# Perceiver block, flash attention over 25088 keys: the probabilities' transposes moved from TensorE to DMA and VectorE

## The chip, the core and the metric

The kernel runs on one core of a Trainium2 chip. The metric is the time of one execution on the device in microseconds; three executions of the kernel before took 2474.32, 2474.45 and 2477.35 us (median 2474.45).

## The reference

Inputs in float32: x [1, 256, 2048] and a context [1, 25088, 2048]. Three residual layers follow each other:

```python
x = x + xattn(layernorm(x), ctx)      # softmax(q @ ctx.T) @ ctx: the context is keys and values at once
x = x + attn(layernorm(x), Wq, bq, Wk, bk, Wv, bv)   # small attention inside each token, 32 heads, 8 kv heads
x = x + ffn(layernorm(x), W_base, b_base, W_gate, A, B)  # base matmul and 2 of 8 low-rank experts
```

The first layer has 256 queries against 25088 keys with 2048 dimensions and takes most of the time; only its loop is changed.

## The kernel before, in words

**Number format.** Every float32 operand is split into a rounded part ("hi", cast by ScalarE) and the difference ("lo", by VectorE or GpSimd). `product` (L1488 ff.) then takes three matmuls, hi x hi, hi x lo and lo x hi, of 128 x 128 by 512 columns (L1491 to L1493).

**Blocks and turns.** The keys are read in 49 blocks of 512. A *turn* is the work of one block, and each engine has its own program of turns, tied by semaphores. The block comes from memory twice: as `quart` (32 x 32 blocks are turned by VectorE, L1081, into the `tr` chunks: 16 chunks of 128 dimensions, the scores' operand) and as `raw` (natural rows, the values' operand, in four pieces of 512 columns).

**TensorE** in one turn: `chunk_scores` for 16 chunks (six matmuls each: two query tiles by three), and between them the weighted sums of the block *before*: eight pieces (two query tiles by four column pieces) of 12 matmuls. PIECE_AFTER (L414) says after which chunk a piece comes; pieces 6 and 7 are late and come after chunks 0 and 1 of the next turn (LATE_AFTER, L415). After chunk 1 and the late pieces stand the eight transposes of the probabilities of the block before (`probs_group`, L1543, four of 128 x 128 for each query tile, into PSUM).

**ScalarE**: the hi cast of each chunk (L770, may be three chunks ahead; a chunk's cast needs the chunk four before to be used up), after that of chunk 3 the exponentials of both query tiles (`softmax`, L783), after that of chunk 5 the hi part of the turned probabilities (L754), and the hi parts of the value pieces (L781): pieces 2 and 3 of the block before after chunks 3 and 7, pieces 0 and 1 of this block after chunks 11 and 15 (ROWS, L804).

**VectorE** in `iteration` (L1159): the row maxima, then for chunks 3 to 18 (16 to 18 are 0 to 2 of the next turn) the difference `lo_chunk` (L1085) and the block transpose of the chunk three ahead (L1081); after chunk 5 the differences of the probabilities (`pt_lo`, L1026), after chunk 7 `rescale` (two operations on 128 x 2 numbers, L1114 and L1116), and after the chunks in ADD_AFTER and ADD_LATE_AFTER (L1141) the additions of finished pieces to `acc` (L1124, L1133). An addition frees the PSUM bank that the piece after next writes.

**GpSimd**: the differences of the value pieces (`lo_piece`, L617, four operations of 128 x 512 each, L621), always in the order 0, 1, 2, 3 of a block. In the first 16 turns after the first it also loads and sums a piece of Wq and stores it (L634 to L643), in the others it sums a window of W_base in every second turn (L649).

**SyncE** issues nearly all loads and stores in order, each with its wait in front (`next_block`, L488). In the last turns it also issues the eight loads of the experts' matrix B (`load_expert`, L521): four after the next-to-last block's loads, four after the load of x for the second layer (`x_nat`), ahead of the last block's pieces 2 and 3.

## Time and profile before

| | |
|---|---|
| median of three executions | 2474.45 us |
| profiled execution, its own time | 2480.7 us |
| its span, first to last instruction | 2478.9 us |
| TensorE (PE) busy | 2444.7 us, 99% |
| VectorE (DVE) busy | 1966.2 us, 79% |
| GpSimd (POOL) busy | 1412.2 us, 57% |
| ScalarE (ACT) busy | 1098.5 us, 44% |
| mean granted TensorE clock | 0.996 |
| mean DMA rate | 210 GB/s |

How to read it: PE is the matmuls, PEld the weight loads that lie beside them, DVE VectorE, ACT ScalarE, POOL GpSimd, SP SyncE; a name with q, as SPq, is an engine's queue, which issues DMAs. Matmuls are pipelined, so the distance between two starts, not the duration of one, is what a matmul costs. L621 is line 621 of the kernel before. Idle time of an engine that is not the bound costs nothing.

### The profile page before, as it was taken

The numbers are of one execution on the slowest core, as the hardware profiler recorded it, in microseconds if no ns is written. First come the engines' busy times: TensorE is split into PE (matmuls) and PEld (weight loads), VectorE is DVE, ScalarE is ACT, GpSimd is POOL, SyncE is SP. The second block draws the span as 40 slices with busy tenths as digits, with TensorE's granted clock in tenths as the row PEclk, the third lists the DMA queues.
The fourth block names the chain that finished last, engine by engine and source line by source line (L and its number), as shares of the span: only waits on it lengthen the run. The fifth ranks groups of instructions, "written<-read, shape, count | busy, mean of one in ns | idle before, by whom it ended". The sixth has DMA issues, their size and how long they took to land. (4 is left out here: it accounts for less than half of the span.)

```text
span 2478.9 us, 36112 instructions
## 1 busy us (share of the span) xinstructions
PE 2444.7 (99%) x11446; PEld 2013.8 (81%) x11446; DVE 1966.2 (79%) x2706; ACT 1098.5 (44%) x1577; POOL 1412.2 (57%) x1052
## 2 busy tenths in 40 slices
PE   6999999999999999999999999999999999999999
PEld 5888888888888888888888888888888888877777
DVE  8888788787888888888888888888888888874456
ACT  4444444444444444444444444444444444433543
POOL 2766666666665655655566565556556555651541
PEclk9999999999999999999999999999999999999999
DMA  9988878888789888889888988888888898789642
GB/s 231 257 221 213 233 203 230 218 208 230 205 231 230 213 204 219 217 220 217 209 220 206 226 217 203 219 223 210 215 217 220 214 216 215 201 187 189 173 119 90
DMA packets 434167, 519.80 MB, mean 210 GB/s; under 512 B 66886, under 2 KB 308550, under 8 KB 431688
## 3 DMA queue, kind: packets, MB, share of 16 engines
q1 hardware_dynamic: 424136, 477.23, 79.0%
q0 software_dynamic: 9984, 41.95, 5.2%
q8 instruction: 28, 0.46, 0.1%
q14 instruction: 19, 0.16, 0.0%
HBM read 488.71 MB, written 30.41 MB: 209 GB/s over the span
## 5 line engine op out<-in xcount | busy, mean ns | idle before, releaser
L621 POOL TENSOR_TENSOR nat_lo<-raw,nat_hi 128x512 fp32r<-128x512 f32 x784 | 1171.0, 1524 | 862.7 <-ACT nat_hi L781 829.7
L1085 DVE TENSOR_TENSOR ch_lo<-tr,ch_hi 128x512 fp32r<-128x512 f32 x784 | 762.6, 973 | 295.5 <-ACT ch_hi L770 291.7
L770 ACT CAST ch_hi<-tr 128x512 fp32r<-128x512 f32 x784 | 481.3, 621 | 797.7 <-PE ps L1493 777.3
L1491 PE MATMUL ps<-ch_hi,xt_hi 128*128 128x512 f32 x1696 | 671.7, 396 | 9.3 <-DVE ch_lo L1085 5.1
L1493 PE MATMUL ps<-ch_hi,xt_lo 128*128 128x512 f32 x1696 | 662.1, 390 | 0.0
L1492 PE MATMUL ps<-ch_lo,xt_hi 128*128 128x512 f32 x1696 | 661.5, 390 | 0.0
L1491 PE MATMUL ps<-nat_hi,pt_hi 128*128 128x512 f32 x1568 | 610.4, 389 | 0.0
L1493 PE MATMUL ps<-nat_hi,pt_lo 128*128 128x512 f32 x1568 | 610.3, 389 | 0.0
L1492 PE MATMUL ps<-nat_lo,pt_hi 128*128 128x512 f32 x1568 | 610.0, 389 | 0.0
L1081 DVE STREAM_TRANSPOSE tr<-quart 128x512 f32<-128x512 f32 x784 | 547.5, 699 | 2.4 <-DMA quart<-in_ctx_dram 2.2
L781 ACT CAST nat_hi<-raw 128x2048 fp32r<-128x2048 f32 x196 | 374.4, 1910 | 207.5 <-PE ps L1493 186.2
L1491 PEld LDWEIGHTS ps<-ch_hi,xt_hi 128*128 128x128 f32 x1696 | 319.1, 188 | 76.5 <-issue 6.5
L1493 PEld LDWEIGHTS ps<-ch_hi,xt_lo 128*128 128x128 f32 x1696 | 319.0, 188 | 67.5
L1492 PEld LDWEIGHTS ps<-ch_lo,xt_hi 128*128 128x128 f32 x1696 | 319.3, 188 | 63.0
L1491 PEld LDWEIGHTS ps<-nat_hi,pt_hi 128*128 128x128 f32 x1568 | 294.4, 188 | 61.4 <-DVE pt_lo L1026 0.4
L1493 PEld LDWEIGHTS ps<-nat_hi,pt_lo 128*128 128x128 f32 x1568 | 294.3, 188 | 61.1
L1492 PEld LDWEIGHTS ps<-nat_lo,pt_hi 128*128 128x128 f32 x1568 | 294.4, 188 | 60.9
L1124 DVE SCALAR_TENSOR_TENSOR acc<-acc,alpha,ps 128x512 f32<-128x512 f32 x240 | 170.0, 708 | 16.2 <-PE ps L1493 16.1
L1133 DVE SCALAR_TENSOR_TENSOR acc<-acc,alpha,ps 128x512 f32<-128x512 f32 x144 | 103.2, 717 | 4.4 <-PE ps L1493 4.4
L754 ACT CAST pt_hi<-ps 128x512 fp32r<-128x512 f32 x98 | 52.8, 589 | 116.3 <-PE ps L1500 116.3
L1026 DVE TENSOR_TENSOR pt_lo<-ps,pt_hi 128x512 fp32r<-128x512 f32 x98 | 63.1, 685 | 49.0 <-ACT pt_hi L754 49.0
L787 ACT ACTIVATE probs<-ps,neg_max 128x512 f32<-128x512 f32 x98 | 67.2, 686 | 73.8 <-DVE neg_max L1106 73.8
(202 smaller groups left out, 1387.0 us busy)
## 6 DMA issues: line engine op xcount, KB each, us to landing
quart<-in_ctx_dram SPq DMA_DIRECT2D x392, 512.0 KB, 8.4
raw<-in_ctx_dram SPq DMA_DIRECT2D x196, 1024.0 KB, 8.2
wq_in<-in_L_attn_Wq_dram POOLq DMA_DIRECT2D x16, 1024.0 KB, 6.3
win<-in_L_ffn_W_base_dram SPq DMA_DIRECT2D x64, 256.0 KB, 6.8
tr<-wt_dram POOLq DMA_DIRECT2D x64, 256.0 KB, 3.6
wt_dram<-stage SPq DMA_DIRECT2D x32, 256.0 KB, 5.6
wt_dram<-stage_b SPq DMA_DIRECT2D x32, 256.0 KB, 10.3
wq_dram<-wq_out POOLq DMA_DIRECT2D x16, 256.0 KB, 2.3
```

Of the source, the lines that this page charges most:

```text
L621: last = pool.tensor_tensor(nat_lo[:, j, t], raw[:, j % 2, t], nat_hi[:, j, t].bitcast(F32), ALU.subtract)
L770: act.copy(ch_hi[:, c % RING_CH, :], tr[:, c % RING_TR, :]).then_inc(chunk_hi, 1)
L781: act.copy(nat_hi[:, j], raw[:, j % 2]).then_inc(nat_hi_ready, 1)
L787: act.activation(probs[:, q, :], ps[:, SCORE_BANK + TT * new + q, :], ACT.Exp, bias=neg_max[:, new, q:q + 1], accum_out=row_sum[:, q:q + 1 ...
L1026: dve.tensor_tensor(dst, src, hi.bitcast(F32), ALU.subtract).then_inc(lo_drained, 1)
L1081: dve.transpose(tr[:, c % RING_TR, :].rearrange("p (r i) -> p r i", i=SQ), src).then_inc(chunk_transposed, 1)
L1085: dve.tensor_tensor(ch_lo[:, c % RING_CH, :], tr[:, c % RING_TR, :], ch_hi[:, c % RING_CH, :].bitcast(F32), ALU.subtract).then_inc(chunk_s ...
L1124: dve.scalar_tensor_tensor(piece, piece, alpha[:, 1 - turn.parity, q:q + 1], ps[:, out_bank(v, turn.over), :], ALU.mult, ALU.add).then_inc ...
L1133: dve.scalar_tensor_tensor(piece, piece, alpha[:, turn.parity, q:q + 1], ps[:, out_bank(v, False), :], ALU.mult, ALU.add).then_inc(acc_upd ...
L1491: pe.matmul(out_, a_hi, b_hi, start=start, stop=False)
L1492: pe.matmul(out_, a_hi, b_lo, start=False, stop=False)
L1493: return pe.matmul(out_, a_lo, b_hi, start=False, stop=stop)
```

## The change

In turns 2 to 48 of the loop (`by_dma`: neither first, second nor the closing one) the probabilities are no longer turned by TensorE. ScalarE writes them with their columns permuted in groups of 32. GpSimd, on its own DMA queue, issues eight DMAs from `probs` to a new buffer `quads`, each of 128 rows of 128 numbers, that deal the 128 partitions out to groups of 32 partitions (`move_next_probs`). VectorE then does two 32 x 32 block transposes of 128 x 512 back into `probs` (`turn_probs`); their output goes to every fourth word. The hi and lo parts are taken from `probs` in SBUF and no longer from PSUM. GpSimd's order becomes pieces 0 and 1, the moves for the next turn, pieces 2 and 3. In front of the moves of each tile stands a one-column multiply (`beat`) that waits for the exponential.

With it change: the places of TensorE's pieces 0 and 1 (after chunks 6 and 8, before 5 and 7), of two casts and two additions, the order of addition, turned probabilities and chunk transpose in VectorE's loop; piece 0 waits for the first tile's probabilities only, and piece 1 for the second's. As `quads` takes the room of the experts' B matrix, all eight of its loads now come after `x_nat` and wait for the last probabilities.

```diff
...
         b_nat = put(at_b, "b_nat", [P, DC, ER])
+        quads = put(at_b, "quads", [P, TT, QR, P])
         x1_sum = put(at_b, "x1_sum", [P, TT, QKC])
...
         ones = sb("ones", [P, P])
+        beat = sb("beat", [P, 1])
         early_exp = sb("early_exp", [P, 1])
...
         probs_ready = sem("probs_ready")
+        beat_done = sem("beat_done")
+        probs_moved = [sem(f"probs_moved{q}") for q in range(TT)]
         alpha_ready = sem("alpha_ready")
...
                 self.second = isinstance(i, int) and 2 * i + 1 + step == 1
+                self.by_dma = not (self.first or self.second or self.over)
...
-        PIECE_AFTER = {5: 0, 7: 1, 9: 2, 11: 3, 13: 4, 15: 5}
+        PIECE_AFTER = {6: 0, 8: 1, 9: 2, 11: 3, 13: 4, 15: 5}
         LATE_AFTER = {0: 6, 1: 7}
...
             next_block(REST[0], LAST_M)
-            for e in range(EXPERTS // 2):
-                load_expert(e)
...
             sp.dma_start(x_nat[:], x_dram).then_inc(x_again, 16)
-            for e in range(EXPERTS // 2, EXPERTS):
+            sp.wait_ge(lo_drained, G_PT + TT * (NB - 1))
+            for e in range(EXPERTS):
                 load_expert(e)
...
                 pool.memset(neg_max[:, parity, :], -LOWEST).then_inc(max_ready, 1)
+            pool.memset(beat[:, :], 1.0).then_inc(beat_done, 1)
             pool.memset(denom[:, :], 0.0).then_inc(denom_ready, 1)
...
                     lo_piece(j, turn.times(PIECES, j + 1))
+
+            def move_next_probs(turn, q):
+
+                pool.wait_ge(beat_done, turn.times(TT, q - 1))
+                pool.wait_ge(probs_ready, turn.times(TT, q + 1))
+                pool.tensor_tensor(beat[:, :], ones[:, 0:1], ones[:, 0:1], ALU.mult).then_inc(beat_done, 1)
+                for b in range(QR):
+                    pool.dma_start(quads[b * SQ:(b + 1) * SQ, q], probs[:, q, b * P:(b + 1) * P]).then_inc(probs_moved[q], 16)
...
                     split_block(Turn(i, step), range(2))
+                    for q in range(TT):
+                        move_next_probs(Turn(i, step), q)
                     pool.wait_ge(wq_loaded, i * 32 + 16 * step + 16)
...
                     sum_win(m)
-                split_block(turn)
+                split_block(turn, range(2))
+                if not turn.last:
+                    for q in range(TT):
+                        move_next_probs(turn, q)
+                split_block(turn, range(2, PIECES))
...
                 act.wait_ge(max_ready, turn.times(TT, q + 1))
-                act.activation(probs[:, q, :], ps[:, SCORE_BANK + TT * new + q, :], ACT.Exp,
+                to, of = probs[:, q, :], ps[:, SCORE_BANK + TT * new + q, :]
+                if turn.by_dma:
+                    to = to.rearrange("p (b t j) -> p t b j", b=QR, t=KT)
+                    of = of.rearrange("p (t b j) -> p t b j", b=QR, t=KT)
+                act.activation(to, of, ACT.Exp,
                                bias=neg_max[:, new, q:q + 1],
...
             def probs_group(turn, q):
-                hi_group(turn.times(TT, G_PT + q - TT), q, pt_hi[:, q], bank4(q))
+                if turn.by_dma:
+                    act.wait_ge(out_ready, turn.times(8, 6 + q + 1 - 16))
+                    hi_group(turn.times(TT, G_PT + q - TT), q, pt_hi[:, q], probs[:, q].rearrange("p (t m) -> p t m", t=KT))
+                else:
+                    hi_group(turn.times(TT, G_PT + q - TT), q, pt_hi[:, q], bank4(q))
...
             SECOND_ROWS = {15: 0, 18: 1}
-            ROWS = {11: 0, 15: 1}
+            ROWS = {12: 0, 15: 1}
...
+            def turn_probs(turn, q):
+
+                dve.wait_ge(probs_moved[q], turn.times(16 * QR, -16 * QR))
+                dve.transpose(probs[:, q].rearrange("p (t i a) -> p t a i", t=KT, a=QR),
+                              quads[:, q].rearrange("p a (t j) -> p t a j", t=KT)).then_inc(group_done, 1)
+
             def probs_group(turn, q):
-                lo_group(turn.times(TT, G_PT + q - TT), pt_lo[:, q], bank4(q), pt_hi[:, q])
-
-
-
-            ADD_AFTER = {9: 0, 11: 1, 13: 2, 15: 3, 17: 4}
+                src = probs[:, q].rearrange("p (t m) -> p t m", t=KT) if turn.by_dma else bank4(q)
+                lo_group(turn.times(TT, G_PT + q - TT), pt_lo[:, q], src, pt_hi[:, q])
+
+
+
+            ADD_AFTER = {10: 0, 12: 1, 13: 2, 15: 3, 17: 4}
             ADD_LATE_AFTER = {3: 5, 5: 6, 7: 7}
...
                     lo_chunk(turn.times(DC, c), c)
+                    if c in ADD_LATE_AFTER and lagging:
+                        add_late_piece(turn, ADD_LATE_AFTER[c])
+                    if c == (7 if turn.second else 5) and not turn.first:
+                        if turn.by_dma:
+                            for q in range(TT):
+                                turn_probs(turn, q)
+                        for q in range(TT):
+                            probs_group(turn, q)
                     n = c + AHEAD
...
                         transpose_chunk(turn.times(DC, n), n, turn.times(16 * QR, 16 * QR * (n // DC)))
-                    if c == (7 if turn.second else 5) and not turn.first:
-                        for q in range(TT):
-                            probs_group(turn, q)
-                    if c in ADD_LATE_AFTER and lagging:
-                        add_late_piece(turn, ADD_LATE_AFTER[c])
                     if c == 7 and not turn.first:
...
                     pe.wait_ge(lo_drained, turn.times(TT, G_PT - 1 + (v > 0)))
+                elif turn.by_dma and v < TT:
+                    pe.wait_ge(lo_drained, turn.times(TT, G_PT - 1 + v))
                 elif v == 0:
...
                         late_piece(turn, LATE_AFTER[c])
-                    if c == (3 if turn.second else 1) and not turn.first:
+                    if c == 3 and turn.second:
                         for q in range(TT):
```

## Rows read from the trace of the kernel before

**Rows 1.** The page: engines' busy time with instructions, and the SyncE DMA queue.
```profile
PE 2444.7 (99%) x11446; PEld 2013.8 (81%) x11446; DVE 1966.2 (79%) x2706; ACT 1098.5 (44%) x1577; POOL 1412.2 (57%) x1052
...
q1 hardware_dynamic: 424136, 477.23, 79.0%
```

**Rows 2.** Time line of TensorE: start, duration in us, line, operation, count.
```profile
1521.12 1.03 PE L1500 MATMUL ps<-ident,probs 128*128 128x128 f32 x8
...
1523.37 0.39 PE L1491 MATMUL ps<-ch_hi,xt_hi 128*128 128x512 f32 x1
...
1544.90 0.39 PE L1493 MATMUL ps<-nat_hi,pt_lo 128*128 128x512 f32 x1
...
2010.63 0.47 PE L1491 MATMUL ps<-ch_hi,xt_hi 128*128 128x512 f32 x1
...
2055.07 0.48 PE L1491 MATMUL ps<-ch_hi,xt_hi 128*128 128x512 f32 x1
```

**Rows 3.** Waits, 100 to 2150 us: total, times, longest.
```profile
DVE ch_lo L1085 <- ACT ch_hi L770: 281.5, 257, 4.1
```

**Rows 4.** Time line of VectorE in the same turn, idle time before in brackets.
```profile
1519.30 1.47 DVE L1085 TENSOR_TENSOR ch_lo<-tr,ch_hi 128x512 fp32r<-128x512 f32 x1 [0.27 <-ACT ch_hi L770]
1520.70 0.70 DVE L1081 STREAM_TRANSPOSE tr<-quart 128x512 f32<-128x512 f32 x1
...
1527.62 1.19 DVE L1114 TENSOR_TENSOR denom_s<-denom,alpha 128x2 f32<-128x2 f32 x1
1528.85 1.21 DVE L1116 TENSOR_TENSOR denom<-denom_s,row_sum 128x2 f32<-128x2 f32 x1
```

**Rows 5.** Groups by form: busy us, mean ns of one, idle time before.
```profile
L1085 DVE TENSOR_TENSOR ch_lo<-tr,ch_hi 128x512 fp32r<-128x512 f32 x784 | 762.6, 973 | 295.5 <-ACT ch_hi L770 291.7
...
L1026 DVE TENSOR_TENSOR pt_lo<-ps,pt_hi 128x512 fp32r<-128x512 f32 x98 | 63.1, 685 | 49.0 <-ACT pt_hi L754 49.0
```

**Rows 6.** Time line of ScalarE in the same turn.
```profile
1513.72 0.19 ACT L787 ACTIVATION_READ_ACCUMULATOR probs<-ps,neg_max 128x1 f32 x1
...
1518.65 0.62 ACT L770 CAST ch_hi<-tr 128x512 fp32r<-128x512 f32 x1 [2.23 <-PE ps L1493]
...
1525.51 1.91 ACT L781 CAST nat_hi<-raw 128x2048 fp32r<-128x2048 f32 x1
```

**Rows 7.** Time line of GpSimd: same turn, and four DMA issues after the loop.
```profile
1515.98 5.94 POOL L621 TENSOR_TENSOR nat_lo<-raw,nat_hi 128x512 fp32r<-128x512 f32 x4 [5.67 <-ACT nat_hi L781]
...
2218.22 2.14 POOL L685 DMA_DIRECT2D tr<-wt_dram  x4
```

**Rows 8.** The page's DMA issues: count, KB each, median us to landing.
```profile
tr<-wt_dram POOLq DMA_DIRECT2D x64, 256.0 KB, 3.6
wt_dram<-stage SPq DMA_DIRECT2D x32, 256.0 KB, 5.6
...
wq_dram<-wq_out POOLq DMA_DIRECT2D x16, 256.0 KB, 2.3
```

**Rows 9.** Groups by form: strided outputs (L639, L923) and a plain one (L758).
```profile
L639 POOL TENSOR_TENSOR wq_in<-wq_in 128x512 f32<-128x512 f32 x16 | 17.7, 1104 | 0.0
...
L758 ACT COPY att_t<-ps 128x512 f32<-128x512 f32 x16 | 9.3, 580 | 0.0
...
L923 ACT COPY v_t<-ps 64x256 f32<-64x256 f32 x8 | 5.0, 630 | 0.1
```

**Rows 10.** Time lines of SyncE's queue, GpSimd and TensorE around the last block.
```profile
2133.36 7.83 SPq L522 DMA_DIRECT2D b_nat<-in_L_ffn_B_dram  x4
...
2156.55 12.10 SPq L522 DMA_DIRECT2D b_nat<-in_L_ffn_B_dram  x4
...
2172.95 0.43 SPq L436 DMA_DIRECT2D raw<-in_ctx_dram  x1
...
2182.90 10.51 POOL L621 TENSOR_TENSOR nat_lo<-raw,nat_hi 128x512 fp32r<-128x512 f32 x8 [7.12 <-ACT nat_hi L781]
...
2193.96 0.39 PE L1491 MATMUL ps<-nat_hi,pt_hi 128*128 128x512 f32 x1
```

## The prediction

> **What bounds the kernel now.** I read the page first: engines' busy time, the DMA queues, the granted clock. TensorE is busy 99% of the span and the queue of SyncE alone takes 79% of the 16 DMA engines [rows 1]. Then TensorE's time line over one turn, because a busy share does not say whether the matmuls follow each other without a gap. They do: from the matmul at 1523.37 to the one at 1544.90 there are 95 starts, 0.2266 us each [rows 2], at a granted clock near 1. A turn (one block of 512 keys) has 16 chunks x 6 and 8 pieces x 12 = 192 matmuls, 192 x 0.2266 = 43.51 us. The turn itself, from the chunk 2 matmul at 2010.63 to the same one at 2055.07, is 44.44 us [rows 2]. The 0.93 us between are the eight transposes and the slower restart behind them. So in the loop TensorE is the only bound; the other engines wait for it (VectorE for ScalarE's casts 281.5 us, and these for TensorE's freed chunks) [rows 3].
>
> I count times from S, the first matmul of chunk 0 of a turn. The transposes start 36 matmuls later, S + 8.16, and do so at 1521.12 [rows 2], so in the traced turn S = 1512.96.
>
> **Part 1: the eight transposes go.** Turns 2 to 48 are changed, 47 of them: 47 x 0.93 = 43.7 us less on TensorE, if nothing makes it wait. The first two and the closing turn keep them.
>
> **Part 2: the new way of the probabilities.** ScalarE's second exponential is through at 1513.91, S + 0.95 [rows 6], the first 0.86 earlier, S + 0.1. The permuted views cost ScalarE nothing that I count: runs of 32 words, same number of elements. GpSimd, whose piece 1 is done before S, now issues two small multiplies and eight DMAs. Four back to back took 2.14 us [rows 7]; with about 0.1 for each multiply (my guess, no row shows it) the last issue starts at S + 4.1 and ends at S + 4.7. The landing: 2.3 us for the SBUF store on this queue, 3.6 for a load on it [rows 8]. So the last block lands at S + 6.4 to 7.7. Behind these issues wait, on GpSimd, the differences of piece 2, before at 1515.98 = S + 3.0 [rows 7], now at about S + 5, until S + 11. TensorE needs piece 2 only after chunk 13, and the reload of the raw buffer behind it has over 10 us of cover, so the 2 us are hidden. In the 16 turns with the Wq sums, these come behind the moves too and push piece 2 to S + 12; the raw reload then comes about 3 us late for its cast, and the idle time of GpSimd before piece 1 takes that up.
>
> **Part 3: VectorE.** This is where the gain can be lost. TensorE without transposes reaches chunk 8 after 84 matmuls, S + 19.03 (before: after chunk 7, piece 1 and piece 0, far later), because pieces 0 and 1 now stand behind chunks 6 and 8. VectorE's chain to the difference of chunk 8 begins with that of chunk 5, which can't start before chunk 1 is used: 1519.30 = S + 6.34 [rows 4]. Then, by start-to-start times (an instruction's duration less 0.07 that the next one overlaps):
> - the chunk 5 difference 1.40 [rows 4]
> - two late additions, the transposes of chunks 8, 9, 10 and the two new ones, seven at 0.70 less 0.07: 7 x 0.63 = 4.41 (the chunk transpose's 0.70 stands for the new ones) [rows 4]
> - the two denominator steps 1.19 and 1.21, to the next start 2.36 [rows 4]
> - five differences: probabilities 0 and 1, chunks 6, 7 and 8. A difference of two SBUF tiles takes 973 ns on average, one with PSUM in it 685 [rows 5]; it is slow when GpSimd runs its own differences (1.47 at 1519.30 with GpSimd busy from 1515.98 [rows 4, 7]). The probabilities' two change from the second kind to the first. Mean 0.90 each: 4.5.
> Sum 12.67, end at S + 19.01, against S + 19.03. Both sides: all five at 0.61, S + 17.6, nothing lost; all five at 1.40, S + 21.5, 2.5 us lost in each turn. I take 0.3 us a turn: the mean sits on the edge, a turn that is early earns nothing and a late one pays in full. 47 x 0.3 = 14.1. The chunk 6 difference (S + 12.7 against S + 13.6) and the addition that frees piece 2's bank (5.44 us after chunk 8 for some 4.7 us of work) have a little room. The blocks are there at S + 7.7 where VectorE asks for the second at S + 9.0: 1.3 us of cover.
>
> The Trainium skill speaks against this part: Vector Engine (DVE) Microarchitecture Reference, section 5.2, says that a port keeps full rate only on runs of two or more adjacent words, and gives 1.71 to 2.51 ns a column for a write that hops at every element, against 1.05. The new transposes write every fourth word; by it the pair would cost 0.7 to 1.5 us more (an estimate from that page). No VectorE row here writes so.
> The rows of other engines disagree: ScalarE's copy with a strided output takes 630 ns for 256 elements where a plain one takes 580 for 512, about double per element; GpSimd's addition at a stride of four words takes 1104 ns for 512, no more than its plain ones [rows 9]. Ends for the two transposes: 0 and +1.4 us. I take 0, as the stride of GpSimd's row is this very one, and keep the other end as a rival.
>
> **Part 4: more traffic.** 1,024 blocks of 512 bytes in a turn, 0.5 MB beside some 9 MB. At queue 1's average of 74 ns a packet (79% x 16 x 2478.9 / 424136 [rows 1]) they take 4.7 us of the 16 engines' 43.5; by bytes, half of it. Shares near 85% become 90 to 96%. I cost it at 0: loads are issued 12 us or more ahead of their use and land in 8.
>
> **Part 5: the eight expert loads.** Four of them move behind x_nat, to the other four. Every one issues in SyncE's queue, and the four took 7.8 us before and 12.1 us there [rows 10]. Behind them stand the loads of the last block's pieces 2 and 3. That of piece 2 was issued at 2172.95 and would be at 2180.8 to 2185.0; with 8 us of landing, 1.9 of cast and half of GpSimd's 10.5 [rows 6, 10] it is ready at 2196 to 2200, where TensorE asked for it at 2193.96 [rows 10]: 2.2 to 6.2 us. Piece 3 follows 5.25 us later where TensorE takes 2.72 for a piece: 2.5 more. Between 0 (the queue drains faster) and 9; I take 6. TensorE has nothing else there, and the layer norm behind it is a chain.
>
> **The sum.** Against the profiled execution, 2480.7 us (span 2478.9): - 43.7 + 14.1 + 6 = - 23.6, 2457.1. That execution is 6.2 us above the median of the runs, 2474.45; there the same sum gives 2450.9, so 2451.
>
> **The rivals.**
> - *All hidden.* VectorE's five differences find GpSimd between instructions (it idles from S + 11 to S + 13.7). Stall 0, end 0 to 6: 2431 to 2437. For it: 2.7 us of idle GpSimd in the middle of the chain. Against: the denominator steps take 1.2 us each whenever GpSimd runs.
> - *The strided write costs its double.* Chain + 1.3; 0.5 of it is given back, since the probabilities' differences then fall into GpSimd's idle time. Stall 0.8 a turn: - 43.7 + 37.6 + 6 = 0, 2474. No change. It is the mechanism of that section 5.2 of the Trainium skill.
> - *The blocks land late, and the kernel gets slower.* Place: VectorE's wait ahead of the first new transpose; queued behind it on VectorE are the differences of chunks 6 to 8, for which TensorE waits. On SyncE's queue a store out of SBUF with rows of 512 bytes lands after 5.6 us [rows 8]. A landing up to 4.9 us costs nothing, at 5.8 the gain is gone; at 7 us the stall is 2.1: - 43.7 + 98.7 + 6, 2535. Against: this queue's own 2.3 and 3.6.
> - That the change does not take the transposes away can't be: the calls are gone from the loop.
>
> **How the numbers follow.** Forecast 0.50, its own range 2437 to 2463 (stall 0.1 to 0.5, end 0 to 9). All hidden 0.18, strided write 0.20, late landing 0.12. A difference under 0.2%, 5 us, can't be told from none. Faster: 0.48 + 0.18 + 0.05 = 0.71. Same: 0.02 + 0.09 = 0.11. Slower: 0.06 + 0.12 = 0.18. The range 2431 to 2486 leaves out the late landing and the edges.
>
> **What would show it.** A turn of 43.5 to 43.9 us between equal matmuls; a gap in TensorE, if any, in front of chunk 8 (or 6), released by VectorE's difference. The new transposes at 0.70 or at 1.2 and more. No idle time of VectorE in front of them: if there is some, released by a DMA, the third rival holds. Landings on GpSimd's queue under 4.9 us. A gap of 5 to 9 us in front of the last block's pieces 2 and 3. Wrong, whatever the sum: TensorE's gaps in the loop standing at another place than chunk 6 or 8, or a gap per turn above 0.8 us without slow transposes.

## The result: slower by 4.1%

| | before | after |
|---|---|---|
| median of four executions | 2475.90 us | 2576.46 us |
| range | 2474.32 to 2478.28 | 2572.92 to 2578.34 |
| profiled execution, its own time | 2480.7 | 2572.9 |
| its span | 2478.9 | 2571.4 |

The ratio is 1.0411 (95% interval 1.0395 to 1.0427). The forecast was 2451, the range 2431 to 2486. The time lies 90 us above the range's upper end.

The page of the changed kernel, engines' busy time, queues and DMA issues (count, KB each, median us to landing). The last line is the tile's view of `quads`:

```profile
PE 2441.9 (95%) x11070; PEld 1979.0 (77%) x11070; DVE 2072.7 (81%) x2800; ACT 1088.6 (42%) x1577; POOL 1609.6 (63%) x1523
...
q1 hardware_dynamic: 424136, 477.23, 75.9%
q0 software_dynamic: 22016, 66.62, 9.0%
...
quads<-probs POOLq DMA_DIRECT2D x376, 64.0 KB, 3.5
...
DMA to landing us min/median/max: 2.0/3.5/8.2
```

Against [rows 1] TensorE has 376 instructions fewer, as meant: 47 x 8. It is now busy 95% of a longer span, so it waits. The moved blocks land in 3.5 us in the median, inside the 2.3 to 3.6 of the forecast, but not all of them: 108 of the 376 take over 5.8 us.

**Where the time went.** VectorE updates the denominator once a turn, so the distance between two `denom_s` instructions is the length of a turn. *Wq turns* are the 16 with a sum over Wq, *later turns* the 25 of the table's third row, which have none and are settled. Over the whole loop:

| stretch | before | after | difference |
|---|---|---|---|
| first 16 periods (nearly all with a sum over Wq) | 708.6 | 774.2 | +65.6 |
| next 4 | 177.7 | 192.1 | +14.4 |
| next 25, mean of one | 44.43 | 44.98 | +13.7 in all |
| last 3 | 125.5 | 131.2 | +5.6 |
| ahead of the first and behind the last | 356.3 | 349.5 | -6.8 |
| span | 2478.9 | 2571.4 | +92.5 |

Of the 92.5 us, 80.0 lie in the first twenty turns. The waits of the changed kernel from 100 to 800 us (total, times, longest) say what these wait for:

```profile
ACT nat_hi L800 <- DMA raw<-in_ctx_dram: 189.7, 41, 10.9
DVE ch_lo L1112 <- ACT ch_hi L789: 166.7, 49, 10.2
POOL nat_lo L626 <- DMA wq_dram<-wq_out: 117.1, 15, 7.9
```

ScalarE waits for raw rows, and its chunk casts queue behind that wait. GpSimd waits up to 7.9 us for its own store of the summed Wq, 15 times. That store had landed in 2.3 us before [rows 8]. The tile's view of `wq_out` after gives minimum, median and maximum:

```profile
DMA to landing us min/median/max: 2.4/8.2/8.3
```

GpSimd and SyncE's queue in such a turn show why (start, duration, instruction, idle time before):

```profile
531.36 0.63 POOL L637 TENSOR_TENSOR beat<-ones 128x1 f32<-128x1 f32 x1 [2.83 <-ACT probs L810]
531.93 2.22 POOL L639 DMA_DIRECT2D quads<-probs  x4
...
536.50 1.53 POOL L653 TENSOR_TENSOR wq_in<-wq_in 128x512 f32<-128x512 f32 x1
...
541.42 0.57 POOL L658 DMA_DIRECT2D wq_dram<-wq_out  x1 [0.68 <-POOL wq_out L656]
549.87 5.93 POOL L626 TENSOR_TENSOR nat_lo<-raw,nat_hi 128x512 fp32r<-128x512 f32 x4 [7.88 <-DMA wq_dram<-wq_out]
...
537.88 1.93 SPq L448 DMA_DIRECT2D quart<-in_ctx_dram  x4
```

The moves push the sums back, and the store is now issued at 541.42, behind the first four quarter loads of a block (512 KB each), which SyncE issues from 537.88 on. In the kernel before the order was the other way round:

```profile
537.20 0.58 POOL L643 DMA_DIRECT2D wq_dram<-wq_out  x1 [0.68 <-POOL wq_out L641]
...
542.32 1.93 SPq L443 DMA_DIRECT2D quart<-in_ctx_dram  x4
```

The DMA queues of the changed kernel behind that store (packets, MB, time of their packets as a share of the 16 engines' time; q1 is SyncE's, q0 GpSimd's) show where it stood, first from 541.5 to 547.4, then from 547.4 to 549.8:

```profile
q1 hardware_dynamic: 1249, 1.24, 112.9%
...
q1 hardware_dynamic: 302, 0.29, 50.6%
q0 software_dynamic: 80, 0.26, 34.9%
```

For 5.9 us no packet of GpSimd's queue moved. Its 0.26 MB, the store, went when the loads were nearly through. So the store takes 5.9 us longer to land, pieces 2 and 3 start at 549.87, the raw buffers come free late, and their reload is late for ScalarE:

```profile
561.10 1.91 ACT L800 CAST nat_hi<-raw 128x2048 fp32r<-128x2048 f32 x1 [9.50 <-DMA raw<-in_ctx_dram]
```

The delay then feeds itself. ScalarE's later chunk casts queue behind this one, VectorE's chain comes late, and with it the next exponentials, the next moves and the next store. TensorE pays mostly ahead of chunk 6: 42.9 of its 48.2 us of waits between 63 and 837 us are for a `ch_lo`. Behind such a gap it also runs slower for a while. The gap in the next turn ends at 592.22, and from 593.77 to 596.76 eight matmuls start 0.43 us apart, which is the 1.2 GHz level, before it is 0.23 again. The granted clock from 100 to 877 us is 0.98; over the same turns before (100 to 807) it was 1.00.

In the later turns the loss is smaller and has another cause. VectorE, GpSimd and TensorE in the turn that begins at 1507.4:

```profile
1513.74 3.29 DVE L1112 TENSOR_TENSOR ch_lo<-tr,ch_hi 128x512 fp32r<-128x512 f32 x1 [0.18 <-ACT ch_hi L789]
...
1517.61 2.02 DVE L1166 STREAM_TRANSPOSE probs<-quads 128x512 f32<-128x512 f32 x2
...
1521.55 0.65 DVE L1112 TENSOR_TENSOR ch_lo<-tr,ch_hi 128x512 fp32r<-128x512 f32 x1
...
1510.46 2.20 POOL L639 DMA_DIRECT2D quads<-probs  x4
1512.67 5.50 POOL L626 TENSOR_TENSOR nat_lo<-raw,nat_hi 128x512 fp32r<-128x512 f32 x4
...
1522.26 0.50 PE L1528 MATMUL ps<-ch_hi,xt_hi 128*128 128x512 f32 x1 [1.10 <-DVE ch_lo L1112]
```

The chunk 5 difference takes 3.29 us, against 1.47 in [rows 4]. It starts 1.07 us behind piece 2 of GpSimd, which is four subtractions of two SBUF tiles in a row. Then the two new transposes take 2.02 us together. The chunk 6 difference ends at 1522.2 and TensorE starts chunk 6 then, 1.10 us late. Of the 835 differences `ch_lo` that VectorE's time line lists singly, 22 take over 3 us (longest 4.8), 16 of them in the 25 later turns; before, none took over 1.8. From 1010 to 2140 us TensorE waits 28 times for a `ch_lo`, 27.9 us in all: 21 times ahead of chunk 6 and 7 times ahead of chunk 8.

A third, smaller cost falls in every second later turn. There SyncE's loads of W_base rows go out just ahead of the moves, which GpSimd issues from 1553.0 on in this turn, and VectorE comes to wait for the moved tiles:

```profile
1552.47 1.85 SPq L462 DMA_DIRECT2D win<-in_L_ffn_W_base_dram  x4
...
1561.53 1.09 DVE L1166 STREAM_TRANSPOSE probs<-quads 128x512 f32<-128x512 f32 x1 [1.43 <-DMA quads<-probs]
```

In such turns the moves take 5 to 8 us to land. VectorE waits for them in 13 places, 12.1 us in all and 2.8 at most.

### The profile page after: what moved, and what is told of

Read it like the earlier page. It is cut to its first block and busy times, and to the rows that moved or that the text cites. A ratio compares the mean times of both kernels' runs of the same rounds, so it can differ in the third digit from the quotient of the medians.

```text
span 2571.4 us, 36064 instructions
## 1 busy us (share of the span) xinstructions
PE 2441.9 (95%) x11070; PEld 1979.0 (77%) x11070; DVE 2072.7 (81%) x2800; ACT 1088.6 (42%) x1577; POOL 1609.6 (63%) x1523
## 5 line engine op out<-in xcount | busy, mean ns | idle before, releaser
L626 POOL TENSOR_TENSOR nat_lo<-raw,nat_hi 128x512 fp32r<-128x512 f32 x784 | 1121.5, 1462 | 633.5 <-ACT nat_hi L800 513.9
L1112 DVE TENSOR_TENSOR ch_lo<-tr,ch_hi 128x512 fp32r<-128x512 f32 x784 | 834.9, 1065 | 328.3 <-ACT ch_hi L789 328.0
L789 ACT CAST ch_hi<-tr 128x512 fp32r<-128x512 f32 x784 | 468.7, 619 | 615.0 <-PE ps L1530 441.6
L1528 PE MATMUL ps<-nat_hi,pt_hi 128*128 128x512 f32 x1568 | 619.9, 395 | 7.8 <-DVE acc L1160 5.3
L639 POOL DMA_DIRECT2D quads<-probs x376 | 207.1, 556 | 0.2 <-issue 0.2
L1151 DVE SCALAR_TENSOR_TENSOR acc<-acc,alpha,ps 128x512 f32<-128x512 f32 x240 | 168.8, 703 | 4.6 <-PE ps L1530 4.3
L773 ACT CAST pt_hi<-probs 128x512 fp32r<-128x512 f32 x94 | 58.4, 621 | 230.4 <-DVE probs L1166 230.4
L637 POOL TENSOR_TENSOR beat<-ones 128x1 f32<-128x1 f32 x94 | 37.6, 400 | 131.2 <-ACT probs L810 130.4
```

Source lines behind the costliest of these rows:

```text
L626: last = pool.tensor_tensor(nat_lo[:, j, t], raw[:, j % 2, t], nat_hi[:, j, t].bitcast(F32), ALU.subtract)
L639: pool.dma_start(quads[b * SQ:(b + 1) * SQ, q], probs[:, q, b * P:(b + 1) * P]).then_inc(probs_moved[q], 16)
L773: act.copy(dst, src).then_inc(hi_drained, 1)
L789: act.copy(ch_hi[:, c % RING_CH, :], tr[:, c % RING_TR, :]).then_inc(chunk_hi, 1)
L1112: dve.tensor_tensor(ch_lo[:, c % RING_CH, :], tr[:, c % RING_TR, :], ch_hi[:, c % RING_CH, :].bitcast(F32), ALU.subtract).then_inc(chunk_s ...
L1151: dve.scalar_tensor_tensor(piece, piece, alpha[:, 1 - turn.parity, q:q + 1], ps[:, out_bank(v, turn.over), :], ALU.mult, ALU.add).then_inc ...
```

## The experiments

All times are medians; every ratio is to the kernel before, run on the same chip beside it (2472.5 to 2477.3 us). (A) and (B) are the two theories of the text in front of a result.

**1. Four runs that change or keep one part.**

*e1.* GpSimd's wait for the store stands behind pieces 2 and 3:

```diff
-                    pool.wait_ge(wq_stored, i * 32 + 16 * step + 16)
                     split_block(Turn(i, step), range(2, PIECES))
+                    pool.wait_ge(wq_stored, i * 32 + 16 * step + 16)
```

> The changed kernel with one line moved: in the 16 turns with the Wq sums GpSimd waits for the landing of the store of wq_out behind pieces 2 and 3, not ahead of them. Theory A (that wait holds the value pieces: the store lands after 8.2 us where it took 2.3, raw loads follow late, ScalarE's casts wait for them, the chunks stop): the Wq turns fall from 48.3 us to about 45, 16 x 3.3 = 53, and most of the 14 us of the four turns behind them: about 2510 us against 2576. Rival B (the added traffic makes the raw loads late): nothing changes there, 2570 to 2580, and the casts still wait for raw loads for some 190 us in that stretch.

Measured: 2668.05 us, ratio 1.0791 (1.0772 to 1.0811). A miss, and a large one: these turns rose to 54 to 56 us. The wait for raw rows is gone, and another has come. GpSimd and VectorE, and the tile's view of `pt_lo` (duration in ns, minimum, median, maximum):

```profile
541.15 9.88 POOL L626 TENSOR_TENSOR nat_lo<-raw,nat_hi 128x512 fp32r<-128x512 f32 x8
...
541.32 10.86 DVE L1053 TENSOR_TENSOR pt_lo<-probs,pt_hi 128x512 fp32r<-128x512 f32 x2
552.11 0.70 DVE L1108 STREAM_TRANSPOSE tr<-quart 128x512 f32<-128x512 f32 x1
...
L1053 DVE TENSOR_TENSOR pt_lo<-probs,pt_hi x94: 656/692/10607, 103.8 to 2334.5; 128x512 fp32r<-128x512 f32 x94
```

While GpSimd runs eight subtractions in a row, VectorE's two differences of the turned probabilities take 10.86 us instead of 1.4. Nearly all of it is the first: a single one takes up to 10.6 us, and is done about when GpSimd's run is. So one instruction of VectorE waited through many of GpSimd's. TensorE then waits 8.70 us ahead of chunk 6, and the granted clock from 100 to 860 us is 0.90. Before the change the probabilities' difference had one operand in PSUM; all 98 of them took 0.65 to 0.69 us.

*e2.* The new transposes write 32 words in a row; the queries of the probabilities then stand in another order (the output is not the reference's):

```diff
-                dve.transpose(probs[:, q].rearrange("p (t i a) -> p t a i", t=KT, a=QR),
+                dve.transpose(probs[:, q].rearrange("p (t a i) -> p t a i", t=KT, a=QR),
```

> The changed kernel, but VectorE's transposes of the probabilities write contiguous runs of 32 words instead of every fourth word; so the query order of the probabilities is left permuted, which changes no duration elsewhere. Theory A (the strided write costs 0.38 us each, and VectorE's chain to chunk 6 decides the turn): transposes 0.70 instead of 1.08, TensorE's gap ahead of chunk 6 down from about 1.1 to 0.4, turns outside the Wq stretch 44.9 to 44.2, total 2576 - 30 x 0.75 = 2553. Rival B (the gap is set by the lock between VectorE's and GpSimd's differences, which absorbs a shorter transpose): transposes 0.70, gap unchanged, total above 2568.

Measured: 2552.02 us, 1.0322 (1.0305 to 1.0340). A hit. The stride is worth 24 us here. Most of it is in the later turns (44.35 on average against 44.98) and at their edges; from the third on the Wq turns stay at 48.3.

*e3.* In the 30 turns that end the loop GpSimd holds piece 2 until VectorE's difference of chunk 5 is done:

```diff
                         move_next_probs(turn, q)
+                    pool.wait_ge(chunk_split, turn.times(DC, DC + 6))
                 split_block(turn, range(2, PIECES))
```

> The changed kernel, but in the 30 turns with the W_base windows GpSimd starts piece 2 only when VectorE's difference of chunk 5 is through. Theory A (that difference takes 3.3 us where GpSimd starts its own just ahead of it, as it waits for two of them, and 0.8 where it does not): it takes 0.65 to 0.8 in every turn, the gap ahead of chunk 6 is gone or below 0.5, these turns go from 44.9 to 43.6 to 44.2, total 2576 - 30 x 1.0 = 2545. Rival B (the wait only moves to the probabilities' differences and chunk 6): same sum of stalls, 2570 to 2585.

Measured: 2555.74 us, 1.0343 (1.0322 to 1.0365), between the two. Later turns fall to 44.66. The slow instruction moves on: in every second turn the two differences of the probabilities now meet piece 2 and take 2.51 us. And VectorE now waits 32.7 us for the moved tiles, against 12.1.

*e4.* The kernel before with the moves alone: GpSimd issues them as in the change, ScalarE's exponentials wait for them, the expert loads stand where the change has them, and nobody reads `quads`. TensorE still turns the probabilities.

> The kernel before with GpSimd's part alone: the multiplies, the eight DMAs per turn into the new buffer (nobody reads it) and GpSimd's new order, ScalarE's exponentials waiting for the moves of the turn before, and the experts' loads at their new place. TensorE keeps its transposes and its order. Theory A (two costs: GpSimd's order in the Wq turns, and VectorE's chain in all): the Wq turns are as slow as in the changed kernel, about 47 to 48.5 us, the others 44.45 as before; total 2476 + 16 x 3.5 + 5 = 2535. Rival B (traffic of the moves): all turns longer by about the same. Rival C (the slow Wq turns need VectorE's new chain too): total within 10 us of 2476.

Measured: 2537.23 us, 1.0259 (1.0242 to 1.0276). A hit. With GpSimd's part alone, the Wq turns take 47.6 us, the store lands in 8.2 (median), and later turns stay at 44.45. So 64 us (2537.23 less 2473.04, the kernel before beside it) come without VectorE's new work. Slow `ch_lo` are here as well, 21 of over 3 us, but from 900 to 2200 us TensorE never waits for one: its own transposes and piece 0 stand ahead of chunk 6 there. So the slow differences follow from where the moves put piece 2, and they cost time only where the transposes no longer cover them.

**2. Is it the store behind the loads?**

*e5.* Sums and store ahead of the moves:

```diff
                     split_block(Turn(i, step), range(2))
-                    for q in range(TT):
-                        move_next_probs(Turn(i, step), q)
                     pool.wait_ge(wq_loaded, i * 32 + 16 * step + 16)
...
                     pool.dma_start(wq_dram[bass.ds(i * (2 * P) + step * P, P)], wq_out[:]).then_inc(wq_stored, 16)
+                    for q in range(TT):
+                        move_next_probs(Turn(i, step), q)
```

> The changed kernel with the three sums over Wq and their store issued ahead of the eight moves instead of behind them. (A) The loss of the sixteen turns with a sum over Wq comes from the store being issued behind SyncE's quarter loads: the landing of the store falls from 8.2 us back to about 2.3, these turns fall from 48.3 us to about 45, the settling turns after them too, and the kernel takes about 2510 us (2576 - 16 x 3.3 - 14). (B) The moves load the queues or the sums wait for something else: landing stays near 8 us, the turns near 48, 2570 to 2580 us.

Measured: 2591.16 us, 1.0466 (1.0446 to 1.0487). The landing did as (A) said, 2.4 us, and the time did not. Now the last moves are the ones issued beside the quarter loads. SyncE's queue, GpSimd, VectorE, and the landing of the two moves issued between 505 and 512:

```profile
504.54 2.17 SPq L448 DMA_DIRECT2D quart<-in_ctx_dram  x4
...
503.73 2.19 POOL L639 DMA_DIRECT2D quads<-probs  x4
...
512.89 1.08 DVE L1166 STREAM_TRANSPOSE probs<-quads 128x512 f32<-128x512 f32 x1 [5.52 <-DMA quads<-probs]
...
quads<-probs POOLq DMA_DIRECT2D x2, 64.0 KB, 6.3
```

VectorE waits 5.52 us for the second tile, and TensorE 4.17 us ahead of chunk 6. This is the rival of the late landing: the moves that went out first took 2.0 to 2.3 us, the last two, behind some of the four loads, 5.0 and 7.5.

*e6 and e10.* The kernel before, its store held back. The edit is e10's; e6 has `times(DC, CH + 1)`:

```diff
+                    pool.wait_ge(chunk_transposed, Turn(i, step).times(DC, DC + CH + 1))
                     pool.dma_start(wq_dram[bass.ds(i * (2 * P) + step * P, P)], wq_out[:]).then_inc(wq_stored, 16)
```

> The kernel before, with TensorE's transposes and no moves; the one edit is that GpSimd waits for the next chunk transpose after the gate of SyncE's quarter loads before it issues the store of the summed Wq. (A) A store that is issued behind the quarter loads lands late by itself: landing 7 to 8.5 us, the sixteen turns 46.5 to 48.5, the kernel about 2530 us (2473 + 16 x 3 + 8). (B) The moves are needed for the late landing: it stays under 4 us, turns under 45, 2474 to 2485 us.

> The kernel before with one wait more: GpSimd issues the store of Wq only when chunk 9 of the next block has been transposed, which is behind SyncE's quarter loads (the run with a wait for chunk 9 of the block before had moved nothing, since that count was long passed). No moves, TensorE's transposes as they were. (A) The store lands in 7 to 8.5 us, the sixteen turns take 46.5 to 49 us, 2515 to 2550 us in all. (B) The moves are needed for it: landing under 4 us, turns under 45, under 2490 us.

e6: 2473.2 us, 0.9997 (0.9985 to 1.0010); my count was a block too low and long passed, so the store did not move (it lands in 2.3 us) and the run says nothing on either theory. e10: 2508.19 us, 1.0136 (1.0114 to 1.0158), below my 2515. The store, now behind the loads, lands so (the tile's view):

```profile
DMA to landing us min/median/max: 2.3/8.4/8.7
```

The turns rise to 46.4 us. So the late landing and its 31 us need neither moves nor new transposes. They are half of e4's 64 us. What e4 has beyond them (the moves' own time on GpSimd, ahead of the sums and of piece 2) no run takes apart.

*e9.* In the Wq turns SyncE issues the quarter loads behind its first raw load, which waits for piece 2:

```diff
+                if m is not None:
+                    next_quarters(turn, 0, quarter(turn.times(KB, KB), 0))
...
                     load_rows(j, ctx_rows(turn.times(KB), j))
+                    if j == 0 and m is None:
+                        next_quarters(turn, 0, quarter(turn.times(KB, KB), 0))
```

> The changed kernel; in the turns with a sum over Wq, SyncE issues the first four quarter loads of a block not before, but behind its first load of ctx rows, which waits for piece 2 and so for the store of Wq. Order and waits of GpSimd stay. (A) Whatever GpSimd's queue is given after the four quarter loads lands behind them: now the store lands in 2.3 to 3 us instead of 8.2, pieces 2 and 3 come 5.5 us earlier, the sixteen turns fall from 48.3 us to 45 or so, and the kernel takes about 2510 us. (B) The store lands late for another reason (the eight moves ahead of it, the load of Wq): 8 us again, 2565 to 2590 us.

Measured: 2606.37 us, 1.0532 (1.0504 to 1.0559). A miss. The store lands in 2.3 us, and the quarters are now late themselves:

```profile
DVE tr L1111 <- DMA quart<-in_ctx_dram: 105.0, 15, 8.2
```

**3. Other mends: the run of subtractions, the stride, both.**

*e8.* Late wait as in e1, with piece 2 held for chunk 5's difference and piece 3 for chunk 8's:

```diff
+                    pool.wait_ge(chunk_split, Turn(i, step).times(DC, DC + 6))
+                    split_block(Turn(i, step), range(2, 3))
+                    pool.wait_ge(chunk_split, Turn(i, step).times(DC, DC + 9))
+                    split_block(Turn(i, step), range(3, PIECES))
                     pool.wait_ge(wq_stored, i * 32 + 16 * step + 16)
-                    split_block(Turn(i, step), range(2, PIECES))
```

> The changed kernel with the wait for the store of Wq behind pieces 2 and 3, as in the run that took 2668 us, but these two pieces are kept apart: piece 2 waits for the difference of the next turn's chunk 5, piece 3 for that of chunk 8. (A) That run lost its time because eight subtractions of GpSimd in a row (9.9 us) let no VectorE instruction with two SBUF inputs finish: with four at a time no difference takes over 4 us, the turns of Wq come to 45 to 46 us and the kernel to 2515 to 2535 us. (B) Something else in the late wait costs the time: the turns stay over 50 us, 2620 us or more.

Measured: 2589.91 us, 1.0462 (1.0441 to 1.0482), between the two theories: 78 us of e1's time are back, yet a difference of the probabilities still takes 5.7 us where it takes 0.69 alone, beside piece 2:

```profile
549.29 5.71 DVE L1056 TENSOR_TENSOR pt_lo<-probs,pt_hi 128x512 fp32r<-128x512 f32 x1 [0.17 <-ACT pt_hi L776]
```

*e7.* Plain write as in e2, with the order of the queries mended where ScalarE and VectorE read the turned probabilities:

```diff
-                    hi_group(turn.times(TT, G_PT + q - TT), q, pt_hi[:, q], probs[:, q].rearrange("p (t m) -> p t m", t=KT))
+                    hi_group(turn.times(TT, G_PT + q - TT), q, pt_hi[:, q].rearrange("p t (i a) -> p t i a", a=QR),
+                             probs[:, q].rearrange("p (t a i) -> p t i a", t=KT, a=QR))
```

> The changed kernel with the order of the queries repaired on the other side: the new transposes write 32 elements in a row, and ScalarE's rounding and VectorE's difference of the turned probabilities read them with a stride of 128 bytes. (A) Only a strided write of a transpose is dear, strided reads are not: as with the plain write alone, 2552 us, turned transposes 0.70 us, differences 0.66. (B) The stride costs in whatever operation has it: the two differences take about 1.1 us each, and the kernel stays at 2570 to 2580 us.

Measured: 2598.03 us, 1.0491 (1.0469 to 1.0514). (B), and worse: the stride costs wherever it stands. Groups by form, of e7 (busy, mean ns):

```profile
L773 ACT CAST pt_hi<-probs 128x512 fp32r<-128x512 f32 x94 | 104.0, 1150 | 200.5 <-DVE probs L1167 200.3
...
L1054 DVE TENSOR_TENSOR pt_lo<-probs,pt_hi 128x512 fp32r<-128x512 f32 x94 | 104.0, 1131 | 25.8 <-ACT pt_hi L773 25.3
...
L1167 DVE STREAM_TRANSPOSE probs<-quads 128x512 f32<-128x512 f32 x94 | 61.9, 687 | 18.6 <-DMA quads<-probs 18.6
```

*e11 and e12.* e9's order, and pieces 2 and 3 held in every turn until chunk 6's difference; e12 writes plainly as well (queries in another order):

```diff
+                    pool.wait_ge(chunk_split, turn.times(DC, DC + 7))
                 split_block(turn, range(2, PIECES))
```

> The changed kernel with the quarter loads behind the store, as in the run on that, and with GpSimd's pieces 2 and 3 held in every turn until the difference of the next turn's chunk 6, which is behind the differences of the turned probabilities. (A) Both losses are these: 2510 us from the first, less 20 us or more from the second (0.5 us in each of some 47 turns), so 2480 to 2492 us, later turns 44.0 to 44.4 us with no difference over 2 us ahead of chunk 6. (B) The time is set by the strided write alone: later turns stay at 44.7 or more, over 2500 us.

> The same, and the new transposes write 32 elements in a row, which leaves the queries of the probabilities in another order: a bound for what the change could bring if the stride cost nothing. (A) The predicted sum of 2451 us holds once landing, lock and stride are gone: later turns 43.5 to 43.7 us, the kernel 2445 to 2465 us, faster than before. (B) The settled turn has another floor near 44 us, 2470 us or more, and the change can't win by any of these mends.

Measured: 2600.49 us, 1.0502 (1.0480 to 1.0525), and 2601.87 us, 1.0526 (1.0492 to 1.0561). Both missed. e9's late quarters are in both. And the hold is too long: GpSimd waits up to 11 us and then runs eight subtractions in 11.9 us, so every second later turn takes 45.7 to 48.1 us, and the ones between them 42.4 to 44.0.

**4. Taking the suspects out.** Nearly every mend so far moved the loss, so the next runs took work away:

```diff
-                for t in range(KT):
+                for t in range(KT if isinstance(ready, int) else 1):
```

That is e14's edit. e13 leaves out the sums over Wq (a quarter of the loaded Wq is stored, and waited for behind pieces 2 and 3); e14 leaves out three of the four subtractions of GpSimd's pieces; e15 is e14 with the plain write; e16 is e15 without the sums.

> The changed kernel without the three sums over Wq: GpSimd stores a quarter of the loaded Wq as it is, does pieces 2 and 3 right behind the moves and waits for the store only then, so that the sixteen turns are arranged as the later ones. (A) The extra loss of these turns (and of the four behind them) is only the wait for the store: they take 44.7 to 45.3 us as the later ones, the raw rows are not waited for, and the kernel takes 2495 to 2505 us (2576 - 80 and a little). (B) The moves themselves disturb these turns, whatever the store: 46 us or more each, 2520 us or more.

> The changed kernel with one of the four subtractions of each of GpSimd's pieces (three quarters of the low parts of the ctx rows are left as they were); sums over Wq, moves and waits stay. (A) VectorE's slow differences come from GpSimd's runs of instructions: no difference takes over 2 us, the later turns fall to 43.9 to 44.2 us (43.51 and what the stride's 0.75 us leaves behind the cover), and the kernel takes 2525 to 2545 us, since the store still lands late. (B) The slow differences have another cause: later turns stay at 44.9, and the kernel at 2560 us or more.

> The same with the new transposes writing 32 elements in a row. (A) Without lock and stride TensorE never waits in the later turns: 43.5 us each, as the sum had it, 2515 to 2535 us in all. (B) TensorE has another limit: 44 us or more.

> The same, and without the sums over Wq as well: landing of the store, lock and stride all gone. (A) These three are the whole error: all turns 43.5 us, and the kernel takes 2431 to 2445 us (2474 - 43.7, and up to 14 at the ends), faster than before. (B) Something unnamed is left: 2455 us or more.

| run | time | ratio | turns 3 to 15 | later turns |
|---|---|---|---|---|
| e13 | 2527.85 | 1.0206 (1.0179 to 1.0232) | 45.43 | 45.25 |
| e14 | 2446.64 | 0.9885 (0.9867 to 0.9903) | 43.52 | 43.52 |
| e15 | 2445.43 | 0.9888 (0.9868 to 0.9907) | 43.5 | 43.5 |
| e16 | 2440.76 | 0.9867 (0.9848 to 0.9885) | 43.52 | 43.52 |

The last two columns are mean lengths. Three readings. The base of the forecast, 43.51 us a turn, was right. With GpSimd's pieces short the strided write costs 1 us in all (e14 against e15, no more than the scatter of the runs) and the late store nothing in a turn: it still lands in 8.2 us in e14, and the turns take 43.52. Neither has a price of its own: it depends on how late GpSimd's pieces and VectorE's chain already are. And in e13, where pieces 2 and 3 do not wait for the store, the Wq turns are the later ones' equals, with a chunk 5 difference of 3.85 us beside piece 2:

```profile
511.16 5.50 POOL L626 TENSOR_TENSOR nat_lo<-raw,nat_hi 128x512 fp32r<-128x512 f32 x4
...
511.65 3.85 DVE L1107 TENSOR_TENSOR ch_lo<-tr,ch_hi 128x512 fp32r<-128x512 f32 x1 [1.58 <-ACT ch_hi L784]
```

My numbers for e13 and e14 were off (2500 and 2535 expected), because I took the three losses to add up.

**5. GpSimd's order put back.** The moves need not be issued by GpSimd. In e17 SyncE issues them ahead of its quarter loads, and GpSimd has its pieces, sums and store in the order of before. All work is done:

```diff
+            def move_probs(turn, q):
+                sp.wait_ge(probs_ready, turn.times(TT, q + 1 - TT))
+                for b in range(QR):
+                    sp.dma_start(quads[b * SQ:(b + 1) * SQ, q], probs[:, q, b * P:(b + 1) * P]).then_inc(probs_moved[q], 16)
...
+                if turn.by_dma:
+                    for q in range(TT):
+                        move_probs(turn, q)
                 next_quarters(turn, 0, quarter(turn.times(KB, KB), 0))
...
-                    for q in range(TT):
-                        move_next_probs(Turn(i, step), q)
```

> The changed kernel, but SyncE issues the eight moves of a turn (it waits for the exponentials ahead of its quarter loads), and GpSimd neither moves nor beats: it does its pieces, the sums over Wq and their store in the order of the kernel before. All work is done and the output is that of the reference. (A) The loss came from what the moves do to GpSimd's order: the store lands in 2.3 us again, pieces 2 and 3 run in front of the differences of chunks 5 and 6, all turns take 43.5 to 44.2 us, and the kernel 2445 to 2468 us, faster than before. (B) SyncE comes late to the moves, or its quarter loads come late behind them: waits of VectorE for the moved quads or for the quarters, turns over 45 us, 2500 us or more.

Measured: 2480.98 us, 1.0045 (1.0029 to 1.0062). From the third on the Wq turns are at 43.6, the store lands in 2.5, no `ch_lo` difference takes over 1.9 us; 95 us of the loss are back (2576.46 less 2480.98). The time lies above the 2468 of (A). Every second later turn is still long, 44.4 to 46.7 us against 43.1. SyncE's queue and VectorE ahead of a long one:

```profile
1550.62 1.88 SPq L462 DMA_DIRECT2D win<-in_L_ffn_W_base_dram  x4
1553.00 5.10 SPq L492 DMA_DIRECT2D quads<-probs  x8
...
1561.35 2.32 DVE L1162 STREAM_TRANSPOSE probs<-quads 128x512 f32<-128x512 f32 x2 [0.85 <-DMA quads<-probs]
```

The moves stand behind the loads of W_base rows. e18 swaps these two, by issuing the moves of such a turn at the end of the turn before's program:

```diff
                 if step == 1:
+                    for q in range(TT):
+                        move_probs(turn, q, TT)
                     for k in (3, 4):
                         sp.wait_ge(wt_stored[k], m * 16 + 16)
                     load_win(m + 1)
```

> As the run with the moves by SyncE, and the four loads of W_base rows, which SyncE issued 2.4 us ahead of the moves in every second one of the later turns, come behind the moves. All work is done. (A) In that run every second later turn took 44.4 to 46.7 us against 43.1 in the others, because the moves landed behind these loads (VectorE waited 0.85 us for the quads in the turn at 1553 us); now all take 43.3 to 44 us, and the kernel 2455 to 2466 us, faster than before. (B) The long turns come from something else (the slow differences beside GpSimd, or the W_base rows are then late for their transposes): 2475 us or more.

Measured: **2454.69 us**, ratio 0.9909 (0.9890 to 0.9929), faster than both kernels, all work done. Later turns take 43.52. Nearly all of the gain is there: these 25 take 22.7 us less than before, while the first 16 take 708.0 us, as before. SyncE's queue, and the landing of the moves:

```profile
1542.85 5.09 SPq L492 DMA_DIRECT2D quads<-probs  x8
1548.30 1.87 SPq L462 DMA_DIRECT2D win<-in_L_ffn_W_base_dram  x4
1550.84 1.91 SPq L448 DMA_DIRECT2D quart<-in_ctx_dram  x4
```

```profile
DMA to landing us min/median/max: 2.1/2.2/5.3
```

Its strided transposes still take 1079 ns each. That they cost nothing here agrees with e15.

## Why the prediction was wrong, step by step

- **Part 1, the transposes.** Right: 43.52 us a turn in e14, e16 and e18, against 43.51.
- **Part 2, the moves.** The issues (2.2 us for four) were right, and so was the landing in the median (3.5 us against 2.3 to 3.6), not its spread: 2.0 to 8.2. The first multiply took about 0.6 us, not 0.1. In the later turns piece 2 starts 5.3 us behind S (1507.39 and 1512.67), where the forecast had about 5.
- **Part 2, what stands behind them on GpSimd: the step that failed.** The prediction had the push of piece 2 "to S + 12" in the Wq turns, costed it with the store's old landing of 2.3 us, and let GpSimd's idle time "take that up". The store had moved past SyncE's quarter loads. It lands after 8.2 us, and piece 2 starts at S + 23.3 (526.62 to 549.87), where it was S + 4.2 before. Of the 11.3 us beyond the forecast 5.9 are the landing, and 4.6 are the first multiply, at S + 4.7 (531.36) and not S + 0.1, since the exponentials are late in a turn that is itself late. Nothing takes that up: the loss is 65.6 us in these turns and 14.4 in the four behind. e4 has it with the moves alone, e10 half of it with a late store alone, and e17, whose piece 2 starts at S + 4.4, is free of it with the order restored. The prediction did ask, for the expert loads, what stands ahead in the queue. It did not ask it for the store.
- **Part 3, the edge.** That the mean sits on the edge was right, and so was the kind of gap: mostly one in a turn, released by a chunk difference. It stands ahead of chunk 6 three times in four (21 of 28), else ahead of chunk 8. The price was 1.5 us a turn (44.98 less 43.51), not 0.3. Two terms were too small. A difference beside GpSimd was bounded at 1.40 and took 3.2 to 4.8 in 22 cases. And the new transposes took 1.08 us each where I had 0.70. In the turn shown the difference of chunk 6 ends at S + 14.8 (1507.39 to 1522.2); the forecast had S + 12.7, against S + 13.6 for TensorE.
- **The strided write.** I went by GpSimd's row in [rows 9], the same stride but another engine; ScalarE's row was the better witness. Vector Engine (DVE) Microarchitecture Reference, section 5.2, of the Trainium skill gives an extra 0.66 to 1.46 ns a column (1.71 to 2.51 less 1.05), for another instruction; the trace agrees, with 0.75 measured, (1081 - 699) / 512. The rival that rested on it had the duration right and the price wrong: 24 us beside a late chain (e2), 1 us beside an early one (e15).
- **Part 4.** Traffic as such cost nothing in the later turns. The DMA share between 850 and 2200 us is 0.87 before, 0.91 after and 0.92 in e18, which carries every byte of the change at 43.52 us a turn.
- **Part 5, the expert loads.** Over-sized: 6 us forecast. The gap ahead of the last pieces is one of 1.43 us at 2293.62. (By its own terms the lower end of that sum for piece 2 is 2.0 us and not 2.2, and the forecast's own range begins at 2435.5 and not 2437. Neither matters.)
- **The rivals.** The late landing was named, for the wrong transfer. For the moves it held in part: 108 of 376 took over the stated 5.8 us, in every second later turn, and VectorE waited 12.1 us for them in all. The Wq store beside them, whose late landing alone cost 31 us in e10, was not named. That the kernel came out slower, as this rival had it, is no merit of the rival's mechanism.

What stays open: why piece 2 holds up a difference of VectorE for 3.3 us in the changed kernel and none for over 1.9 us in e17 and e18. There it starts 2.3 us earlier in the turn (S + 2.9 to 3.0 against S + 5.2 to 5.3), against the same instructions of VectorE. How the two engines' starts must lie for the long wait was not tried by itself.

## What to carry to other kernels

A small transfer that comes to be issued behind large ones can land as late as they do: when an instruction is put ahead of a DMA issue, ask for every issue behind it, on its queue and on the others, what it is now issued behind. In this kernel the new transfers did best on the queue that has time, at a place ahead of the large loads (e18), rather than in front of the work of an engine that others wait for. And where two delays meet on one chain, test them together: undone one at a time, most of the mends here only moved the loss.

## What the runs showed of the hardware

- A 256 KB store on GpSimd's queue landed in 2.3 us when SyncE's four loads of 512 KB came behind it, and in 8.2 to 8.4 (medians) when it was issued behind them (after, e4, e10, e14). In the one shown none of its packets moved for 5.9 us, while SyncE's queue moved 1249. DMA: Bandwidth & Descriptors, section "Queues, rings and completion order", of the Trainium skill has every DMA engine take turns, packet by packet, between the queues that it has work for. The trace does not show such turns here. Whether the store's packets stood ready for the engines in that time, no view shows.
- VectorE's differences of two SBUF tiles beside GpSimd's run of four such subtractions took 1.1 to 1.8 us mostly, and 3.29, 3.85, 4.8 and 5.7 us at worst (after, e13, after, e8); beside eight, one took up to 10.6 (e1). Two operations on 128 x 2 numbers took 1.2 us each beside such a run, and 0.12 and 0.16 where GpSimd was idle (546.14 and 546.30 in the changed kernel). SBUF — State Buffer, section "SBUF: two separate sides", of the Trainium skill has whichever of the two starts first hold the shared ports for its whole instruction. If the other came next, that would bound the wait by one instruction of GpSimd's, 1.3 to 1.5 us (an estimate from that rule and these traces). The traces show waits over several in a row.
- A stride cost time on VectorE, where it wrote and where it read, and on ScalarE: a transpose that writes every fourth word took 1081 ns against 699, a difference that reads with a stride of 32 words 1131 against 719 (means of e7 and the changed kernel), and a cast that does so 1150 against 621. GpSimd's additions at a stride of four words took 1104 [rows 9].
